# A gated cross-attention block in 256 head slots: values weighed one head later, two reciprocals, two x updates and two second parts moved to later places

## The chip, the cores and the metric

The kernel runs on one core of one Trainium2 chip. The metric is device time in microseconds (us) for one launch that computes all 16 batches. The compute engines are TensorE (PE; PEld is its weight load), VectorE (DVE), ScalarE (ACT) and GpSimd (POOL); SyncE (SP) issues the DMAs. Each engine runs its own list of instructions in order and waits on semaphores.

## The reference

Two Flamingo-like layers on x of shape (16, 256, 256) with a context of the same shape, 16 heads of 16 features each:

```
x = x + tanh(g_xattn[0]) * cope_attention(layernorm(x), ctx)      # 16 heads, positions from gates
x = x + tanh(g_ffn[0])   * experts(layernorm(x))                  # 8 experts, top 2, and a shared one
x = x + tanh(g_xattn[1]) * cross_attention(layernorm(x), ctx)
x = x + tanh(g_ffn[1])   * gated_attention(layernorm(x))          # its output scaled by routed gates

def cope(query, attn_logits, pos_emb):
    gates = sigmoid(attn_logits)
    pos = minimum(reversed cumsum of gates, 63)
    logits_int = query @ pos_emb
    return logits_int[ceil(pos)] * w + logits_int[floor(pos)] * (1 - w)     # w = pos - floor(pos)
```

## The kernel before

All 256 heads of the first attention (16 batches x 16 heads, called the core) are a software pipeline of slots. In slot s VectorE makes six masks from the whole part of the positions (`masks`), one comparison (`rises`) and six predicated copies that look up the table (`banks<-masks,banks`, the `MOVES`), then the scan of the next head's gates (`c`), then the sum over steps (`steps`, `negmax`) of head s-1. ScalarE makes in slot s, in this order: `shift16` of this head (L568), the gates and scores of the next (L537 to L547), the exponentials of head s-2 (`core_prob`), then copies out of PSUM, `slope` (L603, which waits for the six copies) and the whole part of the next head's positions (`shift`, L556, for which the next slot's masks wait). GpSimd makes `neg_rest` from `shift16`; the next scan of gates waits for it.

Everything else of a batch (tail of the core attention, experts, cross attention, gated attention) is the side work: one generator per engine, cut by `yield` into 110 pieces for a batch. It runs 20 slots behind the core. The table `PLAN` says for each of 16 slots which pieces run where: a string of groups for TensorE and ScalarE (F before the core's transposes, M before the table product or `slope`, L at the slot's end) and a string of places for VectorE: a digit 0 to 4 is the place behind that copy (0 is behind the first), 5 behind the scan of gates, 6 behind the sum over steps. A seventeenth entry of `PLAN` holds what a batch still has to do in the slot where the next batch begins. Slot s takes entry (s-20) mod 16. Entries 8 and 13 (`MAXIMA`) hold the row maxima of the cross and the gated attention: 16 heads' scores on TensorE and 8 reductions on VectorE (L1265, two heads each). Entries 9 and 14 (`VALUES`) hold most of the second pass: TensorE makes the transposed scores of head h (L1115, L1116) in one of three banks, ScalarE their exponentials (L1198) into a ring of six buffers, and for every four heads TensorE weighs the values (`weigh_values`, L364), which waits for the exponentials of all four. TensorE's scores of head h wait for the exponentials of head h-3. Entries 10 and 15 hold the rest: the last heads, transposes back to tokens (L373), the reciprocal of the sums and the normalised output (L1286, L1287), the output projection (L295) and what follows from it.

The third stream, `ahead`, prepares the core of the next batch: loads, layernorm, projections, and two "second parts" (L319): the rounding rest of keys and of queries, made by VectorE from what ScalarE wrote just before (L311). `AHEAD` says how many of its pieces a slot runs, always at the slot's end, on every engine. The keys' second part lies in slots with s mod 16 = 10, the queries' in those with s mod 16 = 11.

## Time and profile before

| | |
|---|---|
| median of 3 runs | 5130.43 us (5129.69 to 5141.13) |
| the profiled execution's own time | 5137.21 us |
| its span, first to last instruction | 5135.5 us |
| busy share of the span | DVE 78%, PE 67%, ACT 47%, POOL 27% |
| mean granted TensorE clock | 0.722 of full speed |

Times in rows are microseconds from the span's start. The masks of a slot are six instructions of L716, and the first of them is taken as the slot's start. The rows below follow one batch's passage: slot 74 starts at 1391.68, slot 75 at 1414.05, slot 76 (`MAXIMA`) at 1436.82, slot 77 (`VALUES`) at 1460.76, slot 78 at 1474.73, slot 79 at 1497.09; slot 81 (`MAXIMA`) at 1529.14, slot 82 (`VALUES`) at 1551.41, slot 83 at 1566.82, slot 84 at 1589.14 and slot 85 at 1609.04.

### The profile page before, as it was taken

The numbers are of one execution on the slowest core, as the hardware profiler recorded it, in microseconds if no ns is written. First come the engines' busy times: TensorE is split into PE (matmuls) and PEld (weight loads), VectorE is DVE, ScalarE is ACT, GpSimd is POOL, SyncE is SP. The second block draws the span as 40 slices with busy tenths as digits, with TensorE's granted clock in tenths as the row PEclk, the third lists the DMA queues.
The fourth block names the chain that finished last, engine by engine and source line by source line (L and its number), as shares of the span: only waits on it lengthen the run. The fifth ranks groups of instructions, "written<-read, shape, count | busy, mean of one in ns | idle before, by whom it ended". The sixth has DMA issues, their size and how long they took to land.

```text
span 5135.5 us, 64542 instructions
## 1 busy us (share of the span) xinstructions
PE 3439.1 (67%) x21126; PEld 2246.7 (44%) x21126; DVE 3981.5 (78%) x8619; ACT 2429.6 (47%) x5505; POOL 1385.9 (27%) x1125
## 2 busy tenths in 40 slices
PE   3347676766767667676766767667675766767676
PEld 2125354453535435354443535435363443635363
DVE  3699787787978778787887978778797887978753
ACT  2454544545444444444545445444544545455432
POOL 0342322323232232222223222232322223232200
PEclk7558686686867768687686957768586776867686
DMA  4000000000000000000000000000000000000000
GB/s 124 13 5 1 1 11 1 11 1 3 9 1 11 1 11 1 1 11 1 11 1 8 4 1 11 1 11 1 1 11 1 11 1 11 1 1 7 1 7 3
DMA packets 42691, 40.93 MB, mean 8 GB/s; under 512 B 6468, under 2 KB 42342, under 8 KB 42360
## 3 DMA queue, kind: packets, MB, share of 16 engines
q1 hardware_dynamic: 42360, 36.85, 2.3%
q8 instruction: 167, 2.74, 0.2%
q14 instruction: 164, 1.34, 0.1%
HBM read 32.64 MB, written 4.19 MB: 7 GB/s over the span
## 4 chain that ended last, share of the span: by engine, by line
DVE 44%; PE 24%; ACT 14%; issue 13%; POOL 2%; DVEq 0%; POOLq 0%; ACTq 0%; DMA 0%; SPq 0%
DVE banks L725 8%; DVE row_negmax L1265 5%; DVE u L954 4%; PE banks L364 4%; DVE masks L716 4%; PE banks L286 4%; PE banks L273 3%; DVE eg_eth L972 3%; DVE c L687 3%; PE banks L295 2%; DVE o L981 2%; PE banks L328 2%; DVE steps L741 2%; PE banks L802 2%; ACT core_prob L579 2%
## 5 line engine op out<-in xcount | busy, mean ns | idle before, releaser
L725 DVE COPY_PREDICATED banks<-masks,banks 128x448 f32<-128x448 int16 (+5 forms) x1536 | 1030.8, 671 | 35.9
L630 POOL TENSOR_TENSOR steps<-slope,rises 128x512 f32<-128x512 f32 x256 | 301.0, 1176 | 2722.5 <-DVE masks L716 2562.2
L802 PE MATMUL banks<-xn,w 128*128 128x256 f16 x6912 | 872.2, 289 | 88.2 <-ACT h L874 58.3
L802 PEld LDWEIGHTS banks<-xn,w 128*128 128x128 f16 x6912 | 703.0, 104 | 254.9 <-ACT h L874 67.4
L716 DVE TENSOR_SCALAR masks<-shift 128x512 int16<-128x512 int16 x1536 | 334.7, 289 | 156.5 <-ACT shift L556 152.3
L687 DVE TENSOR_TENSOR_SCAN c<-gate,cap 128x514 f32<-128x514 f32 x256 | 371.7, 1452 | 88.2 <-POOL neg_rest L640 87.1
L1265 DVE TENSOR_REDUCE row_negmax<-banks 128x4 f32<-128x1024 f32 x256 | 299.9, 1217 | 141.4 <-PE banks L349 141.4
L815 PE MATMUL banks<-w,a 128*128 128x256 f32 x1152 | 299.7, 407 | 80.2 <-DVE o L981 80.2
L644 POOL TENSOR_TENSOR partial<-partial,core_scores 128x512 f32<-128x512 f32 x256 | 350.4, 1369 | 0.1
L640 POOL TENSOR_TENSOR neg_rest<-shift,c 128x512 f32<-128x512 bf16 x256 | 295.9, 1156 | 183.1 <-ACT shift L568 105.7
L874 ACT ACTIVATE h<-banks,b 128x256 f32<-128x256 f32 x576 | 239.6, 467 | 198.4 <-PE banks L802 197.8
L634 POOL TENSOR_TENSOR partial<-slope,neg_rest 128x512 f32<-128x512 f32 x256 | 324.5, 1267 | 0.0
L451 PE MATMUL banks<-table,core_queries 64*128 64x256 f16 x512 | 122.2, 328 | 283.8 <-ACT slope L603 283.7
L741 DVE TENSOR_TENSOR_SCAN steps<-keep,steps 128x512 f32<-128x512 bf16 x256 | 309.1, 1207 | 0.5
L364 PE MATMUL banks<-a,v 128*32 128x256 f32 x768 | 163.2, 570 | 200.3 <-ACT xT L1198 200.3
L603 ACT ACTIVATE slope<-banks 128x512 f32<-128x512 f32 x256 | 152.4, 595 | 304.7 <-DVE banks L725 304.7
L273 PE MATMUL banks<-ident,core_prob 128*128 128x128 f32 x1024 | 224.1, 359 | 107.4 <-ACT core_prob L579 95.9
L895 ACT ACTIVATE eg_eth<-eg_eth 128x512 f32<-128x512 f32 x144 | 90.6, 630 | 423.7 <-DVE eg_eth L965 423.4
L1115 PE MATMUL banks<-eg_eth,h 64*128 64x256 f16 x1024 | 275.6, 383 | 21.8 <-ACT small L1185 17.5
L595 ACT ACTIVATE core_pT<-banks 128x512 f32<-128x512 f32 x256 | 152.9, 597 | 278.9 <-PE banks L273 278.2
L1116 PE MATMUL banks<-small,pick 64*128 64x256 bf16 x1024 | 278.7, 389 | 0.0
L815 PEld LDWEIGHTS banks<-w,a 128*128 128x128 f32 x1152 | 223.7, 203 | 120.5 <-DVE a L975 86.0
(262 smaller groups left out, 7686.5 us busy)
## 6 DMA issues: line engine op xcount, KB each, us to landing
stage<-in_L_ffn_w SPq DMA_DIRECT2D x16, 512.0 KB, 5.5
ahead<-in_ctx SPq DMA_DIRECT2D x32, 128.0 KB, 2.2
ahead<-in_x SPq DMA_DIRECT2D x32, 128.0 KB, 2.3
u<-in_ctx SPq DMA_DIRECT2D x32, 128.0 KB
x<-in_x SPq DMA_DIRECT2D x32, 128.0 KB
out<-x SPq DMA_DIRECT2D x32, 128.0 KB, 1.8
stage<-in_L_ffn_w SPq DMA_DIRECT2D x8, 256.0 KB, 6.1
stage<-in_L_ffn_sw SPq DMA_DIRECT2D x2, 512.0 KB, 4.2
```

What stands on the lines that cost most here:

```text
L273: last = nc.tensor.transpose(bank[:, c * S + t * P:c * S + (t + 1) * P], src[:, t, c * P:(c + 1) * P], k.ident[:])
L364: last = nc.tensor.matmul(bank[rows, group * S:(group + 1) * S], v[:, c, h * width:h * width + 32], pT[h % len(pT)][:, c, :], start=(c == ...
L630: nc.gpsimd.tensor_tensor(k.steps[:, g % 2], k.slope[:], k.rises[:, g % 2], ALU.mult)\
L634: nc.gpsimd.tensor_tensor(k.partial[:], k.slope[:], k.neg_rest[:], ALU.mult).then_inc(sem["core_steps"], 1)
L644: nc.gpsimd.tensor_tensor(k.partial[:], k.partial[:], k.core_scores[:, g % 3], ALU.add)\
L687: nc.vector.tensor_tensor_scan(k.c[:].rearrange(flat)[:, ::-1], k.gate[:].rearrange(flat)[:, ::-1], k.cap[:].rearrange(flat)[:, ::-1], 0.0 ...
L716: last = nc.vector.tensor_scalar(k.masks[:, n], k.shift[:, :, 0:S], b, None, ALU.bitwise_and)
L725: move = nc.vector.copy_predicated(tab[:, :, 0:S - b], k.masks[:, n, :, 0:S - b], tab[:, :, b:S])
L741: summed = step(nc.vector.tensor_tensor_scan(z.rearrange(flat)[:, ::-1], k.keep[:].rearrange(flat)[:, ::-1], z.rearrange(flat)[:, ::-1], 0 ...
L802: last = nc.tensor.matmul(k.bank[bank][:, f * S:(f + 1) * S], w[:, e, a, c, par, f * P:(f + 1) * P], k.x_parts[:, b, c, :], start=(n == 0) ...
L815: last = nc.tensor.matmul(k.bank[7][:, t * D:(t + 1) * D], k.a[:, e % 2, f, t * P:(t + 1) * P], k.w2[:, e, f, :], start=(f == 0), stop=(f ...
L1265: nc.vector.tensor_reduce(k.row_negmax[:, :, h - 1:h + 1].rearrange("p t h -> p h t"), both, axis=AX.X, op=ALU.max, negate=True).then_inc( ...
```

## The change

Nothing is added or taken out; instructions of VectorE, TensorE and ScalarE stand at other places of their lists.

1. `weigh_values` of heads 0 to 3 is issued after the transposed scores of head 5, no longer after those of head 4; the same for the next two fours (after heads 9 and 13). The last four are weighed where they were.
2. Reciprocals and normalised outputs (L1286, L1287) of both attentions go from place 5 to place 6. The x update of the cross attention (L1034) goes from the end of entry 10 to place 0 of entry 11; the gates' logits of the gated attention (L1300 and on) from the end of entry 15 to place 1 of the next slot, and the rest of its output (L1314 to L1335) in that slot from place 1 to place 3, the core tail's normalised output (L931) from place 3 to 4. Places 3 and 4 lie behind the fourth and fifth copy.
3. The first four reductions of `MAXIMA` stand behind the fifth copy (place 4), where before two stood behind each of the third, fourth and fifth; the last four stand behind the scan (place 5).
4. The second parts (L319) of the next batch leave the ends of slots 10 and 11 (mod 16) and stand behind the fourth copy of the slot after.

```diff
 LAG = 4
-MAXIMA = (5 * "F" + 12 * "M" + 4 * "L", "0" + 4 * "2" + 4 * "3" + 4 * "4" + 8 * "5")
+AHEAD_PLACE = 3
+LATE = (10, 11)
+MAXIMA = (5 * "F" + 12 * "M" + 4 * "L", "0" + 8 * "4" + 12 * "5")
 VALUES = (6 * "F" + 5 * "L", 11 * "5")
-PLAN = [("FMM", "136"), ("FFML", "245"), ("FFL", "135"), ("FFL", "135"), ("FFL", "135"), ("FFML", "1245"),
-        ("FFL", "1245"), ("FFML", "1346"), MAXIMA, VALUES, ("FFFMLL", "000556"),
-        ("FMM", "346"), ("FMM", "046"), MAXIMA, VALUES, ("FFFMLL", "000556"), ("F", "1")]
+PLAN = [("FMM", "346"), ("FFML", "245"), ("FFL", "135"), ("FFL", "135"), ("FFL", "135"), ("FFML", "1245"),
+        ("FFL", "1245"), ("FFML", "1346"), MAXIMA, VALUES, ("FFFML", "00066"),
+        ("FFMM", "0346"), ("FMM", "046"), MAXIMA, VALUES, ("FFFML", "00066"), ("FF", "13")]
...
+    def late(s):
+
+        return s % H in LATE and 8 <= s < G - 1
+
...
                     moved = step(move, wait=False)
+                    if n == AHEAD_PLACE and late(s - 1):
+                        next(ahead, None)
                     some_pieces(places, n)
...
         some_pieces(places, len(MOVES))
-        for _ in range(ahead_pieces(s)):
+        for _ in range(0 if late(s) else ahead_pieces(s)):
             next(ahead, None)
...
         last.then_inc(sem[p + "scoresT"], 1)
-        if h >= 4 and h % 4 == 0:
+        if h >= 5 and h % 4 == 1:
             weigh_values(h // 4 - 1)
```

The kernel's lines move by 2 to 8: before's L319 is L321 after, L716 is L722, L725 is L731, L1265 is L1273, L1034 is L1042, L1115 is L1123, L364 is L366.

**VectorE, the end of slot 75 and slot 76** of one batch (entries 7 and 8), before. `ahead<-banks,bq_cope` is the queries' second part, `banks<-masks,banks` a copy, `row_negmax` a reduction:

```order
L319 SCALAR_TENSOR_TENSOR a<-banks,bq_cross,a 128x256 x2
L319 SCALAR_TENSOR_TENSOR ahead<-banks,bq_cope,ahead 128x256 x2
L716 TENSOR_SCALAR masks<-shift 128x512 x6
...
L725 COPY_PREDICATED banks<-masks,banks 128x2x248
L1265 TENSOR_REDUCE row_negmax<-banks 128x2x2 x2
L725 COPY_PREDICATED banks<-masks,banks 128x2x252
L1265 TENSOR_REDUCE row_negmax<-banks 128x2x2 x2
L725 COPY_PREDICATED banks<-masks,banks 128x2x254
L1265 TENSOR_REDUCE row_negmax<-banks 128x2x2 x2
L725 COPY_PREDICATED banks<-masks,banks 128x2x255
L687 SCALAR_TENSOR_TENSOR c<-gate,cap 128x514
L1265 TENSOR_REDUCE row_negmax<-banks 128x2x2 x2
```

The same place of the same engine after the change:

```order
L321 SCALAR_TENSOR_TENSOR a<-banks,bq_cross,a 128x256 x2
L722 TENSOR_SCALAR masks<-shift 128x512 x6
...
L731 COPY_PREDICATED banks<-masks,banks 128x2x248
L731 COPY_PREDICATED banks<-masks,banks 128x2x252
L321 SCALAR_TENSOR_TENSOR ahead<-banks,bq_cope,ahead 128x256 x2
L731 COPY_PREDICATED banks<-masks,banks 128x2x254
L1273 TENSOR_REDUCE row_negmax<-banks 128x2x2 x4
L731 COPY_PREDICATED banks<-masks,banks 128x2x255
L689 SCALAR_TENSOR_TENSOR c<-gate,cap 128x514
L1273 TENSOR_REDUCE row_negmax<-banks 128x2x2 x4
```

The second part went from the slot's end to behind the fourth copy, two copies went ahead of the first reduction, and the reductions stand in two fours.

**VectorE, from slot 78's scan of gates to slot 79's first copies** (entries 10 and 11), before. `rsum` and `o` are the reciprocal and the normalised output of the cross attention, `x<-banks` its x update:

```order
L687 SCALAR_TENSOR_TENSOR c<-gate,cap 128x514
L1286 RECIPROCAL rsum<-banks 128x16
L1287 TENSOR_TENSOR o<-banks,rsum 128x256
...
L741 SCALAR_TENSOR_TENSOR steps<-keep,steps 128x512
L747 ISA steps,negmax<-steps,partial 128x256
...
L1034 SCALAR_TENSOR_TENSOR x<-banks,tanh_g,x 128x512
L1035 TENSOR_TENSOR x<-x,bo_cross 128x512
L716 TENSOR_SCALAR masks<-shift 128x512 x6
L695 TENSOR_TENSOR rises<-shift 128x512
L725 COPY_PREDICATED banks<-masks,banks 128x2x224
L725 COPY_PREDICATED banks<-masks,banks 128x2x240
```

The same after the change:

```order
L689 SCALAR_TENSOR_TENSOR c<-gate,cap 128x514
L749 SCALAR_TENSOR_TENSOR steps<-keep,steps 128x512
L755 ISA steps,negmax<-steps,partial 128x256
...
L1294 RECIPROCAL rsum<-banks 128x16
L1295 TENSOR_TENSOR o<-banks,rsum 128x256
...
L722 TENSOR_SCALAR masks<-shift 128x512 x6
L697 TENSOR_TENSOR rises<-shift 128x512
L731 COPY_PREDICATED banks<-masks,banks 128x2x224
L1042 SCALAR_TENSOR_TENSOR x<-banks,tanh_g,x 128x512
L1043 TENSOR_TENSOR x<-x,bo_cross 128x512
L731 COPY_PREDICATED banks<-masks,banks 128x2x240
```

The sum over steps now stands ahead of the reciprocals, and the masks, the comparison and one copy of the next slot stand ahead of the x update.

**TensorE, in slot 77** (entry 9), before. The second weighing of values (L364; `ctxT`, `o` and `a` are buffers of exponentials) stands behind head 8's scores and ahead of the core's transposes (L273):

```order
L1115 MATMUL banks<-eg_eth,h 128x256
L1116 MATMUL banks<-small,pick 128x256
L364 MATMUL banks<-ctxT,v 32x256
...
L364 MATMUL banks<-a,v 32x256 x2
L273 MATMUL banks<-ident,core_prob 128x128 x4
L349 MATMUL banks<-core_keys,core_queries 128x256 x2
L451 MATMUL banks<-table,core_queries 128x256 x2
L328 MATMUL banks<-ahead,select 128x256 x4
```

The same after the change:

```order
L1123 MATMUL banks<-eg_eth,h 128x256
L1124 MATMUL banks<-small,pick 128x256
L275 MATMUL banks<-ident,core_prob 128x128 x4
L351 MATMUL banks<-core_keys,core_queries 128x256 x2
L453 MATMUL banks<-table,core_queries 128x256 x2
L330 MATMUL banks<-ahead,select 128x256 x4
...
L366 MATMUL banks<-ctxT,v 32x256
```

The second weighing has left group F for group L, behind head 9's scores, so the core's transposes no longer queue behind it.

## Rows read from the trace of the kernel before

**Rows 1.** Waits of VectorE over the span: total us, times, longest.

```profile
DVE rsum L1286 <- PE banks L373: 208.1, 32, 20.3
DVE row_negmax L1265 <- PE banks L349: 141.4, 32, 6.3
DVE ahead L319 <- ACT ahead L311: 118.0, 32, 6.3
```

**Rows 2.** Windows, one per slot: length, busy PE, PEld, DVE, ACT, POOL; granted clock.

```profile
1391.68:1414.05 22.37, 18.16 (x117) 14.25 (x116) 19.10 (x39) 10.45 (x24) 5.19 (x4) 0.84 0.01 1
...
1474.73:1497.09 22.36, 15.40 (x112) 8.27 (x110) 12.53 (x25) 15.10 (x35) 4.73 (x4) 0.77 0.00 1
...
1566.82:1589.14 22.32, 16.73 (x100) 9.57 (x99) 12.15 (x30) 11.76 (x27) 4.72 (x4) 0.58 0.04 13
```

**Rows 3.** Timeline of VectorE, slots 74 to 76: start, us, instruction, idle before.

```profile
1413.25 0.88 DVE L319 SCALAR_TENSOR_TENSOR ahead<-banks,bk_cope,ahead 128x256 f16<-128x256 f32 x2 [2.81 <-ACT ahead L311]
...
1416.83 0.87 DVE L981 SCALAR_TENSOR_TENSOR o<-banks,cw,o 128x256 f32<-128x256 f32 x2
...
1436.03 0.88 DVE L319 SCALAR_TENSOR_TENSOR ahead<-banks,bq_cope,ahead 128x256 f16<-128x256 f32 x2 [5.51 <-ACT ahead L311]
...
1445.65 2.36 DVE L1265 TENSOR_REDUCE row_negmax<-banks 128x4 f32<-128x1024 f32 x2 [5.25 <-PE banks L349]
1447.92 0.68 DVE L725 COPY_PREDICATED banks<-masks,banks 128x504 f32<-128x504 int16 x1
```

**Rows 4.** Timeline of TensorE in slots 74 to 76.

```profile
1412.07 2.13 PE L815 MATMUL banks<-w,a 128*128 128x256 f32 x8
...
1424.88 3.78 PE L286 MATMUL banks<-xT,wq_cross 128*128 128x256 f32 x8 [0.69 <-ACT xT L1161]
```

**Rows 5.** Timeline of ScalarE in slots 77, 78 and 82.

```profile
1469.34 0.60 ACT L1198 ACTIVATE o<-banks 128x512 f32<-128x512 f32 x1 [2.50 <-PE banks L1116]
...
1472.93 0.60 ACT L595 ACTIVATE core_pT<-banks 128x512 f32<-128x512 f32 x1 [1.26 <-PE banks L273]
...
1480.41 0.60 ACT L1198 ACTIVATE a<-banks 128x512 f32<-128x512 f32 x1 [2.50 <-PE banks L1116]
...
1560.09 0.60 ACT L1198 ACTIVATE o<-banks 128x512 f32<-128x512 f32 x1 [2.50 <-PE banks L1116]
...
1565.01 0.60 ACT L595 ACTIVATE core_pT<-banks 128x512 f32<-128x512 f32 x1 [2.58 <-PE banks L273]
```

**Rows 6.** Timeline of TensorE in slots 82 and 84.

```profile
1552.05 1.93 PE L364 MATMUL banks<-core_pT,core_v 128*32 128x256 f32 x16
...
1598.54 1.12 PE L273 MATMUL banks<-ident,o 128*128 128x128 f32 x4 [4.50 <-DVE o L931]
...
1600.34 3.63 PE L295 MATMUL banks<-wo_cope,h 128*128 128x256 f32 x8 [0.69 <-ACT h L858]
```

**Rows 7.** Timeline of VectorE in slot 78.

```profile
1474.73 1.31 DVE L716 TENSOR_SCALAR masks<-shift 128x512 int16<-128x512 int16 x6 [4.42 <-ACT shift L556]
...
1490.65 0.26 DVE L1286 RECIPROCAL rsum<-banks 128x16 f32<-128x16 f32 x1 [5.56 <-PE banks L373]
...
1491.65 0.42 DVE L1287 TENSOR_TENSOR o<-banks,rsum 128x256 f32<-128x256 f32 x1
...
1495.58 0.75 DVE L1034 SCALAR_TENSOR_TENSOR x<-banks,tanh_g,x 128x512 f32<-128x512 f32 x1 [1.45 <-PE banks L295]
```

**Rows 8.** Timeline of VectorE, slots 82 to 84.

```profile
1566.81 1.31 DVE L716 TENSOR_SCALAR masks<-shift 128x512 int16<-128x512 int16 x6 [5.85 <-ACT shift L556]
...
1587.81 0.19 DVE L1300 TENSOR_TENSOR glog<-banks,brs_row 128x34 f32<-128x34 f32 x1 [0.97 <-PE banks L1134]
...
1597.73 0.75 DVE L931 TENSOR_TENSOR o<-banks,core_rsum 128x256 f32<-128x256 f32 x2
...
1604.45 0.75 DVE L1034 SCALAR_TENSOR_TENSOR x<-banks,tanh_g,x 128x512 f32<-128x512 f32 x1
```

**Rows 9.** Timeline of TensorE in slot 78.

```profile
1493.48 1.99 PE L295 MATMUL banks<-wo_cross,h 128*128 128x256 f32 x8 [0.69 <-ACT h L1207]
```

## Prediction

> **What bounds the kernel now.** I read VectorE's waits first, then windows slot by slot, then the timelines of the slots in which the waits lie. VectorE, the busiest engine, waits in few places, but they come in nearly every batch: for the heads transposed back to tokens (208.1 us), for scores (141.4) and at the second parts (118.0), 32 times each, which is two in a batch [rows 1]. The side work of 15 batches runs beside the core; of the fifteenth the gated attention, and all of the sixteenth, comes after it. Where these waits lie, VectorE is busy for 12.53 of 22.36 us (slot 78) and 12.15 of 22.32 (slot 83), TensorE for 15.40 and 16.73; in slot 74 they are at 19.10 and 18.16 of 22.37 [rows 2]. So the bound there is a chain that goes round VectorE, TensorE and ScalarE, and an edit is worth what it takes out of that chain, not the wait that it touches. I follow the batch of slots 74 to 84.
>
> **Part 1: the second parts (slots 74 to 76).** The keys' part waits 2.81 and takes 0.88 us at the end of slot 74, the queries' waits 5.51 at the end of slot 75 [rows 3]. Taking the first away starts slot 75 by 3.7 earlier. There VectorE next needs the last expert's product, which TensorE ends at 1412.07 + 2.13 = 1414.20 [rows 4]; VectorE read it at 1416.83 [rows 3], would now be there at 1413.1 and waits 1.1 or so. Of 3.7 us 2.6 are left, and the 0.88 of the second part now stand ahead of the layernorm: it ends some 1.7 earlier. From it a serial chain leads on: transposes, the queries' projection of 3.78 us [rows 4], ScalarE's copies, the projection of the next batch, the stacks, the scores. VectorE has nothing in that chain but two second parts, so the first scores come 1.7 earlier, at 1443.9, and not by the 6.4 that VectorE also saves at the end of slot 75. That second saving is hidden: slot 76 starts 1.7 + 6.4 - 0.2 = 7.9 earlier and its scores 1.7, so the wait for scores of 5.25 us [rows 3] grows by 6.2, less 2.2 for the second part and two copies that now lie in it and 1 for the wait at that part: about 8. The moved queries' part waits behind its fourth copy for ScalarE at most a microsecond, and what queues behind it there (two copies, `slope`, the scan) is covered by those 8. **1.7 us** in each of 15 batches. Bounds: nothing more than the 1.7 if the clock stays low; 1.9 more if the projection of 3.78 us ran at the high clock (half of it).
>
> **Part 2: maxima.** Two copies go ahead of the first reduction. A copy is 0.68 [rows 3], and in the row of reductions it costs about 0.55, as two reductions of 2.36 from 1445.65 are followed by the copy at 1447.92 [rows 3] with their ends overlapped. Where VectorE waits for the scores anyway, the copies now lie in that wait, and the slot behind the first reduction is 1.0 shorter. TensorE's scores of heads 12 to 15 wait for reductions 5 and 6, which come behind the scan, so TensorE stays as late as it was. In slot 81 it has nothing else to do after them and the transposed maxima go 1.0 earlier; in slot 76 it has the offset product and a stack of the next batch, which end just when the maxima used to be ready, so nothing is won. **1.0 us** in 14 batches (the fifteenth has its gated attention behind the core), none to 1.0 in the other slot.
>
> **Part 3: values a head later (slots 77, 78, 82, 83).** ScalarE waits 2.50 us for head 5's scores, because TensorE weighs four heads first (1469.34, 1560.09) [rows 5]. With head 5's scores ahead of that, its exponential is done inside the wait, and head 6's starts at the same time instead: 0.5 us won, not 2.5, since the three banks allow no more. The larger gain is behind it: the second weighing leaves group F, 16 products that take 1.93 us at the low clock [rows 6] and about half at the high one, and the core's transposes no longer stand behind it. ScalarE, from 1469.34 on, has three exponentials and a copy, 1.9 us at their spacing of half a microsecond, then copies the transposes: at 1471.2 instead of 1472.93 in slot 77, and at 1562.0 instead of 1565.01 in slot 82 [rows 5]. `slope` and `shift` follow directly, and for them the next masks wait 4.42 and 5.85 us [rows 7, 8], more than these gains. So slot 78 starts 1.75 and slot 83 3.0 earlier. In group L the second weighing is now ahead of head 10, but the third is behind head 13, whose exponential waited 2.50 for it at 1480.41 [rows 5]. At the high clock that wait is worth about 1.5 more than the inserted weighing, at the low clock the two cancel within 0.3. Slot 78 had a granted clock of 0.77, slot 83 one of 0.58 [rows 2]: I take 1.55 for the first and 0.25 for the second. **3.3 us** up to the end of the last head in slots 77 and 78 (15 batches), **3.25** in slots 82 and 83 (14). At the low clock the first is 1.4.
>
> **Part 4: reciprocals and x updates.** In slot 78 the reciprocals wait 5.56 us [rows 7] with the sum over steps (2.1 us) behind them. That sum, and then the masks, the comparison and a copy of slot 79 (2.4 us) now stand in time that was waited. From the normalised output's end (1492.07) to the x update (1495.58) there are 3.5 us of TensorE and ScalarE [rows 7], of which 1.99 is the output projection [rows 9]. Before, the sum, the wait, the update (1.45) and slot 79 up to its first copy took 2.1 + 1.45 + 1.45 + 2.4 = 7.4 us from there; now VectorE does masks to copy (2.4), waits until 3.5 and updates: 4.95. **2.4 us**. Should the projection run at the low clock, as its like in slot 84 (3.63) [rows 6], it is 0.7. In slot 83 the same move takes away, behind the gated attention's output, the sum (2.1), the wait for logits (0.97) and the logits (1.0) [rows 8]: slot 84 starts 4.1 earlier. It then gets the logits (1.0) and three more copies (2.0) ahead of the tail's output, which starts at 1597.73; so that output ends 9.35 + 3.0 = 12.35 us after the slot's start (1589.14). From its end to its x update (1604.45) VectorE had just enough work, 6 us, to hide the projection [rows 8]; with three copies fewer it has 4, and the chain is open: 1.12, 0.69 and 3.63 us on TensorE with ScalarE between [rows 6], 5.5 in all. That makes 17.85 from the slot's start to the update, where it was 15.3. Of 4.1 us **1.5 us** stay, in 14 batches; 3.0 if that projection took 2 us. The store of x and SyncE's load of the next batch's x lie between the last update (which ends with 1597.73) and that x update; 6.7 us were enough for them without a wait [rows 8], and 0.65 + 0.75 + 5.5 = 6.9 are left.
>
> **Sum.** 15 x (1.7 + 3.3 + 2.4) = 111; 14 x (1.0 + 3.25 + 1.5) = 80; the second parts of batch 1, in slots 10 and 11 without side work, about 2 x 2 = 4; nine weighings behind the core at 0.5, 4. Together 199 us. The profiled execution took 5137.2, so 4938; the median of the runs is 7 us below that execution, by it 4931. I predict 4935, between the two. (0.3%, 15 us, is about what a measurement of this kernel can tell from no change.)
>
> **Rivals.**
>
> *Low clock (20%).* TensorE's clock has two levels, 1.2 and 2.4 GHz, and the rows show both for the same work: the 8 products of an output projection took 1.99 us after 0.69 of idleness and 3.63 after 4.50 and 0.69 [rows 6, 9]. If slots 77 to 79 get the low one, parts 3 and 4 there are 1.4 and 0.7: 15 x 3.8 + 80 + 8 = 145, and 4992.
>
> *High clock (15%).* TensorE's idle stretches get shorter, the 4.50 before the tail's output [rows 6] to about 3, so the clock may stay high where it fell: 1.9 more in slot 75 and 1.5 more in slot 84: 199 + 28 + 21 = 248, and 4889. The Trainium skill (TensorE: Matmul & The Clock Gate, Part 1) says that the slow clock is the default and sustained activity releases it; by that rule alone this rival would be the forecast. The trace agrees only in part: slot 83 had 0.58 with TensorE busy for three quarters of it [rows 2].
>
> *It does nothing (3%).* If each wait only came back at the next place (each ends a chain of ScalarE and TensorE), the slots would keep their length, and the time 5137. Against it: in slots 78 and 83 ScalarE and TensorE themselves wait for VectorE or for one another.
>
> *Slower (3%).* Slot 74 and its like are full on TensorE: busy 18.16 us at a granted clock of 0.84 [rows 2], where the slot now shrinks from 22.4 to 18.7. If work pushed together there came at the low level, its 18.16 us would be 18.16 x 0.84 / 0.50 = 30 and the slot 8 us longer. With two such slots in a batch, 16 x 15 - 199 gives 5178. It decides from about 13 us a batch on; it needs the clock to fall where TensorE gets busier, and slot 83 (0.58 with TensorE busy for 16.73 of 22.32 us) shows that a busy slot alone does not rule that out [rows 2].
>
> **How the numbers follow.** The forecast has 59%. Its own range, 4905 to 4965, comes from half a microsecond or so by which each part may be off, 2 us a batch. The range for 8 in 10 reaches to the near end of the high-clock case and 13 us beyond the low-clock case: 4890 to 5005. Faster by over 0.3%: 59 + 20 + 15 = 94%; within it 3%; slower 3%.
>
> **What would show it.** Second parts: no wait at L319's successor, slot 74 at 18.7 us, and the wait for scores in slot 76 at about 8. Maxima: slot 81 a microsecond shorter. Values: ScalarE's waits of 2.50 gone or 2.0 behind head 5, shift waits still 3 to 4 us. Reciprocals: a wait of 3 to 4 in front of them, slot 78 at 16, a new wait of 1 to 3 us for the output projection at the x updates. The prediction is wrong if slot 76's first reduction is not earlier, if the x update waits for more than 3 us, or if the granted clock moves by more than 0.03.

## The result, and the profile after

The changed kernel takes **4905.9 us** (median of 4 runs, 4902.7 to 4915.2) where the kernel before takes 5131.1 beside it: a ratio of 0.956, with a 95% interval of 0.955 to 0.958. 4935 was predicted, so 196 us of gain, and 225 came. (The sum behind it is 199.) The profiled execution has a span of 4906.0, and the span of before was 5135.5.

VectorE's waits over the span (total us, times, longest), after the change, against [rows 1]:

```profile
DVE row_negmax L1273 <- PE banks L351: 151.9, 32, 8.0
DVE rsum L1294 <- PE banks L375: 133.6, 32, 18.1
DVE masks L722 <- ACT shift L558: 85.6, 48, 3.6
DVE c L689 <- POOL neg_rest L642: 82.4, 29, 3.2
DVE x L1042 <- PE banks L297: 34.1, 21, 5.7
...
DVE ahead L321 <- ACT ahead L313: 14.4, 5, 6.6
```

The wait at the second parts is all but gone, the one for the transposed heads is a third smaller, and the one for scores has grown a little, since part of the time saved before it is waited there. The windows of slots 74, 78 and 83 (columns as in [rows 2]):

```profile
1346.68:1365.46 18.78, 14.57 (x108) 11.47 (x107) 18.30 (x36) 8.67 (x20) 5.20 (x4) 0.95 0.00 1
...
1423.73:1441.21 17.48, 13.78 (x116) 6.64 (x114) 10.90 (x23) 10.57 (x24) 4.74 (x4) 0.76 0.00 0
...
1509.06:1526.72 17.66, 13.23 (x102) 6.37 (x101) 11.25 (x24) 10.70 (x24) 4.74 (x4) 0.76 0.02 6
```

Slot 74 lost its wait, and slots 78 and 83 nearly 5 us each, of which slots 79 and 84 take back 3.4 and 0.9 (means over the batches). In slot 83 the granted clock of TensorE rose from 0.58 to 0.76. VectorE's timeline of slots 75 and 76, against [rows 3]:

```profile
1368.71 0.88 DVE L989 SCALAR_TENSOR_TENSOR o<-banks,cw,o 128x256 f32<-128x256 f32 x2 [0.37 <-PE banks L823]
1369.63 1.60 DVE L1032 SCALAR_TENSOR_TENSOR x<-o,tanh_g,x 128x512 f32<-128x512 f32 x1
...
1387.66 0.87 DVE L321 SCALAR_TENSOR_TENSOR ahead<-banks,bq_cope,ahead 128x256 f16<-128x256 f32 x2
...
1396.41 4.82 DVE L1273 TENSOR_REDUCE row_negmax<-banks 128x4 f32<-128x1024 f32 x4 [7.28 <-PE banks L351]
```

The second part waits for nothing in slot 76. The wait for scores behind it is 7.28 us, where 8 were expected. ScalarE in slots 77 and 78:

```profile
1417.41 0.60 ACT L1206 ACTIVATE o<-banks 128x512 f32<-128x512 f32 x1
1420.02 0.60 ACT L1206 ACTIVATE a<-banks 128x512 f32<-128x512 f32 x1 [2.01 <-PE banks L1124]
...
1421.93 0.60 ACT L597 ACTIVATE core_pT<-banks 128x512 f32<-128x512 f32 x1
...
1428.46 0.60 ACT L1206 ACTIVATE ctxT<-banks 128x512 f32<-128x512 f32 x1 [2.23 <-PE banks L1124]
```

Head 5's exponential (1417.41) now follows head 4's, the wait behind it is 2.01 instead of 2.50, and the core's transposes wait for nothing. VectorE in slots 78, 79, 83 and 84, against [rows 7, 8]:

```profile
1423.73 1.31 DVE L722 TENSOR_SCALAR masks<-shift 128x512 int16<-128x512 int16 x6 [3.64 <-ACT shift L558]
...
1439.95 0.26 DVE L1294 RECIPROCAL rsum<-banks 128x16 f32<-128x16 f32 x1 [3.04 <-PE banks L375]
...
1444.72 0.75 DVE L1042 SCALAR_TENSOR_TENSOR x<-banks,tanh_g,x 128x512 f32<-128x512 f32 x1 [1.34 <-PE banks L297]
...
1509.06 1.31 DVE L722 TENSOR_SCALAR masks<-shift 128x512 int16<-128x512 int16 x6 [2.12 <-ACT shift L558]
...
1534.44 0.16 DVE L1334 SCALAR_TENSOR_TENSOR gscale<-gscale,gexp 128x2 f32<-128x2 f32 x1
...
1536.75 0.75 DVE L939 TENSOR_TENSOR o<-banks,core_rsum 128x256 f32<-128x256 f32 x2
...
1542.82 0.75 DVE L1042 SCALAR_TENSOR_TENSOR x<-banks,tanh_g,x 128x512 f32<-128x512 f32 x1 [0.83 <-DVE negmax L755]
```

The waits are near those forecast: 3.04 before the reciprocals (3 to 4 forecast), 1.34 and 0.83 at the x updates (1 to 3). Two of the signs missed: slot 78 is 17.48 us long and not 16, and the masks of slot 83 wait 2.12 and not 3 to 4. The tail's output ends 10.78 us after slot 84 starts (1536.75 + 0.75 less 1526.72), where 12.35 was summed. That row matters below.

### The profile page after: what moved, and what is told of

The parts are those of the page before. It is cut to its first block, busy times and chain, and to the rows that moved or that the text cites. A ratio compares the mean times of both kernels' runs of the same rounds, so it can differ in the third digit from the quotient of the medians.

```text
span 4906.0 us, 64542 instructions
## 1 busy us (share of the span) xinstructions
PE 3332.2 (68%) x21126; PEld 2210.1 (45%) x21126; DVE 3975.6 (81%) x8619; ACT 2426.4 (49%) x5505; POOL 1394.9 (28%) x1125
## 3 DMA queue, kind: packets, MB, share of 16 engines
q14 instruction: 165, 1.34, 0.1%
## 4 chain that ended last, share of the span: by engine, by line
DVE 42%; PE 26%; ACT 13%; issue 13%; POOL 2%; DVEq 0%; POOLq 0%; ACTq 0%; DMA 0%; SPq 0%
DVE banks L731 7%; DVE u L962 5%; PE banks L288 4%; DVE row_negmax L1273 4%; PE banks L366 3%; PE banks L275 3%; DVE masks L722 3%; PE banks L297 3%; DVE eg_eth L980 3%; DVE c L689 3%; DVE o L989 2%; PE banks L330 2%; DVE steps L749 2%; PE banks L810 2%; ACT core_prob L581 2%
## 5 line engine op out<-in xcount | busy, mean ns | idle before, releaser
L731 DVE COPY_PREDICATED banks<-masks,banks 128x448 f32<-128x448 int16 (+5 forms) x1536 | 1030.6, 671 | 36.6
L1273 DVE TENSOR_REDUCE row_negmax<-banks 128x4 f32<-128x1024 f32 x256 | 297.3, 1216 | 154.5 <-PE banks L351 151.9
L722 DVE TENSOR_SCALAR masks<-shift 128x512 int16<-128x512 int16 x1536 | 334.3, 288 | 89.8 <-ACT shift L558 85.6
L646 POOL TENSOR_TENSOR partial<-partial,core_scores 128x512 f32<-128x512 f32 x256 | 361.4, 1412 | 0.1
L366 PE MATMUL banks<-a,v 128*32 128x256 f32 x768 | 158.5, 555 | 177.3 <-ACT xT L1206 177.3
L1123 PE MATMUL banks<-eg_eth,h 64*128 64x256 f16 x1024 | 260.9, 371 | 20.4 <-ACT small L1193 18.3
L330 PE MATMUL banks<-a,select 32*128 32x256 f16 x1024 | 130.9, 354 | 209.0 <-ACT eg_eth L337 113.6
L962 DVE SCALAR_TENSOR_TENSOR u<-banks,b,h 128x256 f32<-128x256 f32 x576 | 249.1, 473 | 21.7 <-PE banks L810 21.6
```

The costliest lines, as they stand in the source:

```text
L366: last = nc.tensor.matmul(bank[rows, group * S:(group + 1) * S], v[:, c, h * width:h * width + 32], pT[h % len(pT)][:, c, :], start=(c == ...
L646: nc.gpsimd.tensor_tensor(k.partial[:], k.partial[:], k.core_scores[:, g % 3], ALU.add)\
L722: last = nc.vector.tensor_scalar(k.masks[:, n], k.shift[:, :, 0:S], b, None, ALU.bitwise_and)
L731: move = nc.vector.copy_predicated(tab[:, :, 0:S - b], k.masks[:, n, :, 0:S - b], tab[:, :, b:S])
L962: nc.vector.scalar_tensor_tensor(k.u[:, par, f, :], k.bank[5 + m % 2][:, f * S:(f + 1) * S], k.b3[:, par, f, e:e + 1], k.h1[:, m % 2, f, : ...
L1273: nc.vector.tensor_reduce(k.row_negmax[:, :, h - 1:h + 1].rearrange("p t h -> p h t"), both, axis=AX.X, op=ALU.max, negate=True).then_inc( ...
```

## Experiments

In the edits below, the digit of a piece in PLAN is the copy of the slot behind which VectorE runs it (0 is behind the first, 5 behind the scan, 6 at the slot's end). Pieces run in one order, so a digit moves whatever piece's turn it is. The table has means over the batches from slot 36 on; a slot is counted from VectorE's first mask comparison to that of the next slot, and the columns name the slots of the batch that this text follows. "Gain" is the difference of medians to the kernel before, run beside it; that kernel's own median lay between 5129.1 and 5136.0 us, so a difference between two gains is uncertain by some 7 us. The slots come from one profiled execution of each kernel, which is up to 13 us (maxima alone) off its median.

A slot's mean also mixes two or three lengths, one for each level at which TensorE runs there. Before the change slot 77 takes 13.8 to 14.0 us in 8 of 14 batches (granted clock 0.65 to 0.70) and 15.1 to 15.3 in 6 (0.50 to 0.54). With the tail's output later, a kernel that has the same instructions in that slot in the same order, it takes 15.1 to 15.3 in all 14 (0.50 to 0.55). A difference of less than a microsecond in the table may be such a change of mixture and not the edit's own.

Two theories were to be told apart. Theory A: the parts add up, and one or two of them were sized too small. Theory B: the excess over the sum comes from TensorE's granted clock when all parts stand together.

| kernel | gain, us | batch | slots 73, 74 | 75, 76 | 77 to 80 | 81 | 82 to 84 |
|---|---|---|---|---|---|---|---|
| before | | 305.4 | 41.8 | 45.5 | 68.8 | 22.3 | 56.9 |
| after | 225 | 290.5 | 38.7 | 45.6 | 65.1 | 21.2 | 49.6 |
| values alone | 107 | 297.9 | 42.0 | 45.2 | 65.7 | 22.3 | 52.4 |
| second parts alone | 30 | 303.4 | 38.7 | 46.9 | 69.0 | 22.3 | 56.4 |
| maxima alone | 1 | 304.2 | 41.8 | 44.7 | 70.2 | 21.2 | 56.2 |
| places alone | 76 | 299.8 | 41.9 | 45.7 | 66.8 | 22.3 | 53.1 |
| update two copies later | 284 | 286.4 | 38.7 | 44.1 | 62.5 | 21.2 | 49.5 |
| three pieces later | 250 | 288.9 | 38.7 | 45.2 | 65.0 | 21.3 | 49.9 |
| two heads later | 230 | 290.4 | 38.7 | 46.0 | 64.4 | 21.3 | 49.8 |
| all places | 294 | 285.8 | 36.3 | 44.8 | 63.7 | 21.2 | 50.9 |
| all places, two heads | 325 | 283.0 | 36.3 | 44.6 | 62.0 | 21.3 | 49.9 |
| norm first | 353 | 281.9 | 36.7 | 43.4 | 62.4 | 21.2 | 49.4 |
| before, tail's output later | -13 | 306.4 | 41.8 | 44.4 | 69.7 | 22.3 | 57.9 |
| before, scales later | -27 | 306.5 | 41.8 | 45.0 | 69.8 | 22.3 | 57.0 |

### Each part alone

Four kernels, each the kernel before with one part of the diff. Values:

```diff
-        if h >= 4 and h % 4 == 0:
+        if h >= 5 and h % 4 == 1:
```

> The kernel before with the values weighed one head later, and nothing else. The sum on record gives this part 15 x 3.3 + 14 x 3.25 + 4 = 99 us, so 5032 against 5131. Theory A, the parts add up and one of them was sized too small: the missing 26 us (225 measured, 199 summed) come in a batch's slots 81 to 84 (8.2 us gained where 5.75 were summed), and this part is where they would be, 125 us and about 5006. Theory B, TensorE's granted clock: the excess is there only when all parts stand together and TensorE's idle stretches are short, so this part alone gives 99 or less. ScalarE's waits of 2.50 us behind heads 5 and 13 are gone or near 2.0 in both.

Second parts: `AHEAD_PLACE`, `LATE`, `late(s)` and the two lines that use them.

> The kernel before with the second parts of the next batch's norm moved a slot on, and nothing else. The sum gives 15 x 1.7 + 4 = 30 us, so 5101. Rival: the wait only moves to the scores of slot 76 and the time stays at 5131. The wait at the second parts should fall from 118 us in 32 to under 30, the wait for scores rise by some 6 us in 15 slots less 1.7.

Maxima: the line of `MAXIMA`.

> The kernel before with two maxima moved behind the fifth copy, and nothing else. The sum gives 14 x 1.0 = 14 us, so 5117; rival: the two copies only displace the wait for scores and nothing is won, 5131. By Theory A the slots 81 of the batches are 1.0 us shorter here as they are with all parts.

Places: the lines of `PLAN`.

> The kernel before with the changed places of the tails alone: reciprocals at the slot's end, x updates and logits a slot on. The sum gives 15 x 2.4 + 14 x 1.5 = 57 us, so 5074; with the output projection of slot 84 at the high clock 78, so 5053. Theory A: the four parts alone sum to about 225. Theory B: they sum to clearly less than 200, since each leaves idle stretches that keep TensorE at its low clock, and the gated projection of slot 84 takes 3.6 us here where it takes 1.98 with all parts.

Measured: 5024.6, 5101.9, 5131.1 and 5055.5 us; ratios 0.979 (0.976 to 0.982), 0.994 (0.992 to 0.996), 1.000 (0.998 to 1.001) and 0.985 (0.982 to 0.988). The gains are 107, 30, 1 and 76: together 214 against 225, where each is known to 8 to 15 us. **So the parts add up within that uncertainty, and Theory B falls as a sum**: it asked for clearly less than 200, and nothing needs all parts to stand together. Its second sign came true all the same: the gated projection of this batch (`wo_gated`), 1.97 us with all parts, takes 3.76 with places alone, as before. The missing gain lies where Theory A put it, in the last slots of the batch: values alone shorten slots 82 to 84 by 4.5 us (3.25 summed) and places alone by 3.8 (1.5 summed). In these slots the parts do not add: the four kernels win 9.4 there, all parts together 7.3.

For the values the reason is TensorE's clock. The windows of slot 82, before and with values alone:

```profile
1551.40:1566.82 15.42, 12.37 (x85) 4.99 (x84) 9.25 (x20) 10.20 (x23) 4.73 (x4) 0.50 0.00 0
```

```profile
1525.79:1536.72 10.93, 7.76 (x70) 3.82 (x69) 9.26 (x20) 10.07 (x23) 4.75 (x4) 0.81 0.00 0
```

The same products of the first weighing stand in TensorE's timelines as follows, before and with values alone:

```profile
1557.15 0.64 PE L364 MATMUL banks<-a,v 128*32 128x256 f32 x2 [2.19 <-ACT xT L1198]
```

```profile
1531.54 0.41 PE L364 MATMUL banks<-a,v 128*32 128x256 f32 x2 [1.58 <-ACT xT L1198]
```

and ScalarE with values alone:

```profile
1533.18 0.60 ACT L1198 ACTIVATE a<-banks 128x512 f32<-128x512 f32 x1 [0.73 <-PE banks L1116]
...
1534.89 0.63 ACT L595 ACTIVATE core_pT<-banks 128x512 f32<-128x512 f32 x1
```

Before, slot 82 of this batch ran wholly at the low level (0.50). With values alone the weighing is granted the high one, so ScalarE waits 0.73 behind head 5 and not 2.0. It copies the core's transposes 9.10 us after the slot's start (1534.89 less 1525.79) where it was 13.61; the sum had 3.0 for these 4.5.

The shorter idleness ahead of the weighing is not the cause. In this batch the level rose some 2 us before the weighing began, ahead of that idleness. In the kernel before, the weighing stands behind the same 2.19 us of idleness in all 13 batches that have it, and ran at the high level in four of them and at the low one in nine. With values alone it ran high in 11 of 13; the two low ones stand behind 1.35 and 2.22 us. What the edit changed is how often the level is high. At the low level through the whole slot, slot 82 takes 15.4 us before and 12.4 in the kernels with the values one head later where that occurs (five batches of the one with all places, one of the one with the update later): 3.0 less, as summed. As a mean over the batches slot 82 went from 14.9 to 11.4 (granted clock 0.56, then 0.71) and slot 83 from 22.0 to 21.1.

The maxima's own slot 81 is 1.0 shorter, as summed. Slot 76 is 0.9 shorter with the two copies inside its wait, and slot 77 0.9 longer at either level (14.9 and 16.2 us, where they were 14.0 and 15.3): nothing is won there, as summed. The rest of the 1.4 that slots 77 to 80 lose in the table is mostly that slot 77 is at the low level in more batches (9 of 13 where it was 5, the last batch aside). The trace has a gain of 1.2 us a batch, the medians (10 runs from 5114 to 5139) can't tell it from none.

### Who holds the second scale's product

Places alone win more than summed in slot 84. Ahead of the tail's output stands a product that took 1.19 us before, and 0.16 now. VectorE, before:

```profile
1594.40 1.19 DVE L1326 SCALAR_TENSOR_TENSOR gscale<-gscale,gexp 128x2 f32<-128x2 f32 x1
```

GpSimd, before:

```profile
1594.31 1.26 POOL L644 TENSOR_TENSOR partial<-partial,core_scores 128x512 f32<-128x512 f32 x1
```

VectorE and then GpSimd with places alone:

```profile
1574.47 0.16 DVE L1326 SCALAR_TENSOR_TENSOR gscale<-gscale,gexp 128x2 f32<-128x2 f32 x1
...
1576.77 0.75 DVE L931 TENSOR_TENSOR o<-banks,core_rsum 128x256 f32<-128x256 f32 x2
...
1582.43 0.75 DVE L1034 SCALAR_TENSOR_TENSOR x<-banks,tanh_g,x 128x512 f32<-128x512 f32 x1 [0.41 <-DVE negmax L747]
```

```profile
1571.92 1.26 POOL L644 TENSOR_TENSOR partial<-partial,core_scores 128x512 f32<-128x512 f32 x1
```

Before, the product of 2 elements a partition ends at 1595.59, as GpSimd's does at 1595.57. With the logits ahead of it, it comes 1.3 us after GpSimd's end. Was it held? Two kernels on the kernel before. The first:

```diff
-        ..., ("FFFMLL", "000556"), ("F", "1")]
+        ..., ("FFFMLL", "000556"), ("F", "3")]
```

> The kernel before with one place changed: the experts' scales of the gated attention, up to the tail's output, stand behind the fourth copy of slot 84 and not behind the second. If the second scale's product (1.19 us, its like 0.16) is held by GpSimd's operation that ends with it, it takes 0.16 here, and two copies more ahead of the tail's output (1.4 us) cost 0.1 to 0.4, not 1.4; the x update behind it comes 0 to 1 us earlier, since two copies fewer stand ahead of it: 5131 less 0 to 14. If it is not held, its 1.19 stays and slot 84 is as long or up to 1 us longer: 5131 to 5145.

This did not do what its expectation says. The batch's own first piece in that slot has place 1 too, so one piece still ran there, and by turn it was the scales; the digit moved the tail's output alone two copies on. 5147.7 us, ratio 1.0025 (1.001 to 1.004), slot 84 longer by 1.07 of the 1.4 that two copies take: it prices a delay of that output, and says nothing on the hold. So the other digit had to go as well:

```diff
-PLAN = [("FMM", "136"), ...
+PLAN = [("FMM", "346"), ...
-        ..., ("F", "1")]
+        ..., ("F", "3")]
```

> The kernel before with the expert scales of the gated attention two copies later in slot 84, together with the tail's output and the piece behind it; the logits stay in slot 83. If GpSimd's operation holds the second scale's product (1.19 us), it is now free and takes 0.16: the tail's output ends 0.3 us later than before and not 1.4, and the x update, with the projection 4.9 us behind, comes 0.4 to 0.8 earlier: slot 84 at 19.1 to 19.5, 5 to 11 us less than before. If the product is long by itself, the output ends 1.4 later and the slot is 0.3 to 1.1 longer (the tail's output alone two copies later made it 1.07 longer): 4 to 15 us more.

5156.4 us, ratio 1.005 (1.003 to 1.006), slot 84 longer by 1.0: slower, against the forecast by the hold. (Slot 84 accounts for 14 of the 27 us. Slots 77 to 80, which the edit leaves alone, are 1.0 longer too, slot 77 at the low level in all batches but one.) VectorE's timeline of slot 84 tells why:

```profile
1597.02 1.62 DVE L1317 TENSOR_TENSOR gexp<-gexp,gsum 128x30 f32<-128x30 f32 x2
...
1599.67 0.16 DVE L1326 SCALAR_TENSOR_TENSOR gscale<-gscale,gexp 128x2 f32<-128x2 f32 x1
```

and GpSimd's:

```profile
1597.36 1.26 POOL L644 TENSOR_TENSOR partial<-partial,core_scores 128x512 f32<-128x512 f32 x1
```

The second scale's product is free (0.16), so its 1.19 was no property of it. But the two products of L1317, which took 0.68 with places alone, now stand beside GpSimd's operation and take 1.62, and end at 1598.64 where it ends at 1598.62. The hold stays and catches whoever is there. I had not thought of that, and priced the edit as if the hold were gone.

### Three pieces later: the same hold elsewhere

Many of the long holds are in the experts. VectorE and GpSimd in slot 71 of the changed kernel:

```profile
1294.08 1.64 DVE L980 SCALAR_TENSOR_TENSOR eg_eth<-eg_eth 128x512 f32<-128x512 f32 x1
1295.75 1.64 DVE L983 SCALAR_TENSOR_TENSOR a<-xT,eg_eth 128x512 f32<-128x512 f32 x1
```

```profile
1294.04 1.12 POOL L642 TENSOR_TENSOR neg_rest<-shift,c 128x512 f32<-128x512 bf16 x1 [0.17 <-POOL partial L636]
1295.13 1.71 POOL L646 TENSOR_TENSOR partial<-partial,core_scores 128x512 f32<-128x512 f32 x1
```

```diff
-..., ("FFL", "135"), ("FFL", "135"), ("FFML", "1245"), ("FFL", "1245"), ...
+..., ("FFL", "445"), ("FFL", "135"), ("FFML", "4445"), ("FFL", "4445"), ...
```

> The changed kernel with three places of the experts' pieces moved: in slots 71, 73 and 74 of a batch the piece that stood behind the second copy stands behind the fifth. In these slots two of VectorE's operations with both inputs in SBUF take 1.63 us each where they take 0.69 elsewhere, and in that time GpSimd has its own operations running. Theory A: they are held by GpSimd's operation; five copies later GpSimd is done, each falls to about 0.7 to 0.95, and each of the three slots is 1.5 to 1.9 us shorter, since VectorE is busy throughout there: 16 x 5 = 80 us less than the changed kernel, about 4826. Theory B: the time is their own or TensorE bounds these slots: the waits come back elsewhere and the time stays at 4906 within 15.

4884.5 us, 21 less than the changed kernel and not 80. The groups of these two lines, of the changed kernel and of this one (busy us, mean ns):

```profile
L983 DVE SCALAR_TENSOR_TENSOR a<-xT,eg_eth 128x512 f32<-128x512 f32 x144 | 142.0, 986 | 5.0
L980 DVE SCALAR_TENSOR_TENSOR eg_eth<-eg_eth 128x512 f32<-128x512 f32 x144 | 140.4, 975 | 0.0
```

```profile
L983 DVE SCALAR_TENSOR_TENSOR a<-xT,eg_eth 128x512 f32<-128x512 f32 x144 | 99.6, 692 | 5.0
L980 DVE SCALAR_TENSOR_TENSOR eg_eth<-eg_eth 128x512 f32<-128x512 f32 x144 | 98.3, 683 | 0.0
```

Theory A is right on the hold: 84.5 us of VectorE's time are gone from these two lines, and slot 71 is 1.4 shorter. Of the 84.5, 16 came back in the operation just ahead of them (L978). In slots 73 and 74 a wait took its place, since three pieces now stand back to back and the third needs what ScalarE makes from the second:

```profile
DVE u L962 <- ACT h L882: 34.0, 31, 1.1
```

### Filling the new waits

```diff
-AHEAD_PLACE = 3
+AHEAD_PLACE = 4
-        ("FFMM", "0346"), ...
+        ("FFMM", "2346"), ...
```

> The changed kernel with the cross-attention's x update two copies later in slot 79 (behind the third copy, not the first) and the queries' second part behind the fifth copy of slot 76's like, not the fourth. The x update waits 2.2 us for the projection, with nothing behind it that could run; two copies of 0.68 fill that: 1.4 x 15 = 21 us less. The second part one copy later lets the layernorm of slot 75 end 0.88 earlier: 13 us less. Together 4906 - 34 = 4872. Rival: the logits' chain behind these updates is covered by other waits, and the time stays within 15 of 4906.

4850.2 us, 56 less than the changed kernel. Slots 77 to 80 are 2.5 us shorter and slots 75, 76 1.5, more than the 1.4 and 0.9 expected. Of the 2.5, slot 79, where the update stands, gave 1.6 and slot 78 gave 1.2, although none of its instructions moved. In the changed kernel slot 78 takes 17.5 to 17.8 us in 11 of 14 batches, here in 2 and else 14.3 to 16.0; in the kernel with all places, which has the same later update, in 10 again. So some 17 of the 56 us came from a change of mixture that no step of the edit's own sum explains, and that is gone again in the kernel with all places. The x updates' wait fell from 34.1 us (10.2 of it behind the core) to:

```profile
DVE x L1042 <- PE banks L297: 15.5, 8, 5.7
```

Next, the values two heads later on the changed kernel:

```diff
-        if h >= 5 and h % 4 == 1:
+        if h >= 6 and h % 4 == 2:
```

> The changed kernel with the values weighed two heads later than before, not one. The first head's delay won 107 us alone. If ScalarE's chain of exponentials still waits for the weighing (1.3 to 2.0 us behind head 5 now), another 0.5 us in each of four slots of a batch is to be had: 30 us less, 4876. Rival: the products weighed later now stand between the last scores and the transposes, which the core needs, and half a group is lost there: 4906 to 4930.

4904.1: no change. Slots 78 and 83 gave 1.9 and 1.6, slots 79 and 84 took back 1.2 and 1.5 and slots 76 and 82 0.7 together, and the wait for the output projection grew:

```profile
DVE x L1042 <- PE banks L297: 54.8, 21, 5.2
```

Then the edits together. The two later pieces of slots 73 and 74 stand behind the scan here ("4455" for "4445"):

> The changed kernel with the three edits together that the last runs measured: in slots 71, 73 and 74 of a batch the piece behind the second copy stands behind the fifth, and now the third piece of slots 73 and 74 behind the scan, so that ScalarE's tanh and copy (the wait of 1.13 us that had come there) lie beside a copy and the scan; the cross-attention's x update two copies later; the queries' second part one copy later. If the earlier slots' hold was what made them long, slots 73 and 74 are now 1.5 us shorter each as slot 71 was (1.4): 15 x 3 = 45 us beyond the two gains of 56 and 22 measured apart, so 4906 - 56 - 22 - 45 = 4783. If slots 73 and 74 are bound by TensorE, which is busy most of them, only the two gains are there: 4828.

> The kernel of all the moved places, with the values weighed two heads later than before the change and the cross-attention's x update behind the fourth copy. Two heads alone gave slots 78 and 83 1.9 and 1.6 us less and slots 79 and 84 1.2 and 1.5 more, where the x update waited 3.85 us for the projection. If a further copy fills that wait, 1.2 us a batch are kept: 15 to 20 us below the kernel of all the moved places. If the projection bounds slot 79 whatever stands in the wait, the two are equal within 10.

The first took 4835.5 us, ratio 0.942 (0.940 to 0.944), 52 more than expected. Slots 73 and 74 are 2.4 us shorter, so TensorE does not bound them at the length that they had; but slots 75 and 76 are 0.7 longer than with the update alone, 77 to 80 1.2 (slot 78 alone 1.3), and 82 to 84 1.4. Two windows of this kernel, slots 74 and 83:

```profile
1329.87:1347.37 17.50, 14.59 (x104) 11.16 (x103) 16.94 (x36) 9.28 (x23) 4.73 (x4) 1.00 0.01 2
...
1490.24:1508.26 18.02, 15.45 (x101) 7.35 (x100) 11.34 (x24) 10.44 (x24) 4.74 (x4) 0.53 0.01 2
```

The granted clock is 1.00 in slot 74 (0.95 in the changed kernel) and 0.53 in slot 83 (0.76). As a mean over the batches slot 83 has 0.60 here and 0.76 in the changed kernel, slot 75 0.72 and 0.80. So part of the gain probably went back in products at the low level: that is argued from these clocks, not measured apart, and that the shorter slots cause it is not shown either. With two heads it took 4803.7 us, 32 less: the wait of 54.8 is now filled.

```profile
DVE x L1042 <- PE banks L297: 22.5, 11, 5.7
```

Last, one edit more on that kernel:

```diff
-        ("FFL", "4455"), ("FFML", "1346"), MAXIMA, ...
+        ("FFL", "4455"), ("FFML", "1146"), MAXIMA, ...
```

> The kernel with all places moved and values weighed two heads later, and one edit more: in slot 75 the layernorm stands right behind the x update, not two copies further on. The chain that leads from the layernorm by transposes, projections and stacks to the first scores of slot 76 bounds these two slots: VectorE waits 8.1 us for the scores there. Two copies of 0.7 fewer ahead of the chain make the scores 1.4 earlier, 15 times: 21 us less, 4783, with the wait for scores at 6.7 to 7.1. Rival: the stacks on ScalarE, which stand behind the core's own copies, or GpSimd's operations bound the scores: the wait stays at 8 and the time at 4804. Rival: TensorE's clock falls elsewhere as it did when slots 73 and 74 became shorter, and half of the 21 us is given back.

**4783.3 us, ratio 0.932 (0.930 to 0.934)**: the 21 us expected, and the fastest of all, 123 us below the changed kernel. Slots 75 and 76 are 1.3 shorter, and the clock did not fall elsewhere (slot 83 has 0.66 and then 0.68). The wait for scores in the two last kernels fell by 1.7 a batch, a little more than the 1.0 to 1.4 expected:

```profile
DVE row_negmax L1273 <- PE banks L351: 163.7, 32, 8.7
```

```profile
DVE row_negmax L1273 <- PE banks L351: 138.8, 32, 7.6
```

## Why the prediction was right, and where its sum was short

Summed and measured by stretch, the forecast came out better than its terms. A batch got 14.9 us shorter, where 13.2 were summed: 3.0 in slots 73 to 76 (1.7 summed), 3.7 in slots 77 to 80 (5.7 summed), 8.3 in slots 81 to 84 (5.75 summed). The 2.0 too few in the second stretch hid part of the 3.8 too many in the others; that the time came out only 29 us below the forecast is in this part luck.

**Part 1** was right in size and mechanism: 1.7 a batch summed, 1.66 measured alone (65.74 for slots 74 to 76, 67.40 before), slot 74 at 18.8, the wait for scores at 7.3. The chain from the layernorm to the scores bounds these slots; the last experiment says so again.

**Part 2** was right for slot 81 (1.0). It was right as well that nothing is won in slot 76, but the way was another: slot 76 did get 0.9 shorter, and slot 77 lost the same 0.9. This is why slots 73 to 76 gave more than their term and slots 77 to 80 less.

**Part 3** was right for slots 77 to 80 (3.3 summed; 3.1, as 68.79 less 65.73). For slots 82 to 84 the term was mis-sized: 3.25 summed, 4.5 measured alone. The step was the core's transposes "at 1562.0" and the 0.25 for slot 83: both took the low level, where the rows of this batch stood at it, and with the edit most batches have the high one in part of these slots (3.6 us off slot 82, 0.9 off slot 83 as means). At the low level the 3.0 holds (15.4 us to 12.4). From slot 255 to the end it took 271.8 us with values alone and 280.7 before, where 4 us were summed for the nine weighings; but kernels whose edits change nothing there took 276.3 to 280.3, so some 4.5 to 9 of it is theirs.

**Part 4** was near for slots 78 and 79 (2.4 summed, 2.2 measured alone). In slots 83 and 84 its first step held (4.1 us off slot 83; 3.9 measured), and the second was mis-sized: "12.35 us after the slot's start" for the end of the tail's output. With places alone it ends 10.77 after it (1576.77 + 0.75 less 1566.75). Of the 1.58, 1.03 is the hold at L1326, which I read as work, and about 0.7 is a third copy that I counted, where two were added: the tail's output (L931) stood behind the second copy of slot 84 and stands behind the fourth, and not, as the text on the change has it, behind the fourth and then the fifth. Against these, 0.35 is a new hold (the two products of L1306 take 0.74 there, and took 0.39). The chain from that output to the x update was taken at 5.5 and took 4.9. The projection behind it stayed at the low level with places alone, 3.42 us in this batch, as taken, so the 3.0 that stood as the other bound came by another way. Places alone also took 5.5 us more behind the core (286.2 against 280.7), for which the sum had nothing; the changed kernel, with the same places, took 274.6, so that no cost of them shows there.

**The rivals.** Of the high-clock one a part came: not the projection of slot 75 (3.51 us in this batch, 3.78 before) nor that of slot 84, but slots 82 and 83. The granted clock of the profiled execution rose by 0.031 (0.722 to 0.753), just past the 0.03 that the prediction named as a sign of being wrong; the four runs of the changed kernel have 0.746 to 0.753. By its own sign, then, the clock was not the small matter that it had been taken for. The rule of the Trainium skill (TensorE: Matmul & The Clock Gate, Part 1) is that sustained activity releases the high clock. The rows do not let one forecast by it: the weighing of slot 82 ran at both levels behind the same products and the same idleness, and in slot 83 of the kernel with all places the clock fell to 0.53 with TensorE busy for 15.45 of 18.02 us.

What stays open: what sets TensorE's level in a slot from one batch, and one kernel, to the next (slots 78, 82 and 83 above all), and with it most of what the update two copies later won beyond the 34 us summed.

## What to carry to other kernels

When a wait goes, sum the chain that bounds the stretch, not the wait: the second parts had 118 us of waits, and taking them out won 30. Before an instruction's duration goes into a sum, compare it with its like: where it is longer in one place, look at what the neighbouring engine does there, for it may be a wait that no list of waits shows, and that moves to the next instruction rather than going away. A new wait that an edit leaves behind is the place for the next edit: one digit and `AHEAD_PLACE` won 56 us, a quarter as much again as the whole change, though not all of it by the wait that they filled. And before a slot's mean is compared between two kernels, list its length batch by batch: where it takes two values, the edit may only have changed how often each comes.

## What the runs showed of the hardware

VectorE's operations with both inputs in SBUF are held while GpSimd works on SBUF, and the profile shows it as a longer operation, not as a wait: 1.64 us for 0.68 (128x512), 1.19 for 0.16 (128x2), each ending with GpSimd's or half a microsecond behind it. GpSimd is held too (1.71 for 1.26 in slot 71). Two with a single input in SBUF and their output there were held too (L978 in the kernel with three pieces later, 0.87 for 0.43, and L256 before the change, 0.87 for 0.17 in 15 of 48). Reductions, copies under a mask into PSUM, and operations that read PSUM kept their time beside it. In the changed kernel's trace no operation of VectorE that ran with GpSimd idle is more than 0.03 us above the middle value of its like, so no excess is seen there without GpSimd. One operation does not fit: `rises`, with both inputs in SBUF (int16), takes 0.41 to 0.42 us in all 256 slots, 253 of them beside GpSimd.

All holds together took 215 us of VectorE before and 208 after the change. The largest sum of one line, in no experiment touched, is the scan of gates: 78 of its 256 in the changed kernel run beside a GpSimd operation that began before them, and take 1.85 us as a middle value where the other 178 take 1.22; that is 58 us (busy us, mean ns):

```profile
L689 DVE TENSOR_TENSOR_SCAN c<-gate,cap 128x514 f32<-128x514 f32 x256 | 371.0, 1449 | 83.6 <-POOL neg_rest L642 82.4 <-ACT gate L542 1.2
```

The change took 14.4 us of such holds away at the second scale's product (16 times 1058 less 161 ns) and made 11.4 new ones where the cross-attention's bias is added, in the changed kernel (busy us, mean ns), where both rows took 692 ns before:

```profile
L1043 DVE TENSOR_TENSOR x<-x,bo_cross 128x512 f32<-128x512 f32 x16 | 22.5, 1403 | 0.6
L1043 DVE TENSOR_TENSOR x<-x,bo_cope 128x512 f32<-128x512 f32 x16 | 11.1, 692 | 0.6
```

The Trainium skill (SBUF — State Buffer, Who interferes with whom) states this: VectorE and GpSimd share a pair of ports, a VectorE instruction with two SBUF inputs contends with GpSimd's reads, one in a 2-port mode as well, and the loser blocks fully. The rows agree in kind and, `rises` aside, in which operations are spared; whether the two single-input operations ran in such a mode no row shows.

TensorE's granted clock is not a property of a slot's own work: in one execution of the kernel before, the weighing of slot 82 ran at the high level in four batches and at the low one in nine, with the same products ahead of it and the same 2.19 us of idleness. What decides is not shown.
